# Late mixing weights in pieces of four degrees, and the linear weights moved to the head of SyncE's queue

## What is computed

```python
def _L0_conv_ref(x, w1r, w1i, w2r, w2i):          # w*: (32 in, 32 out, 32 degrees, 32 orders)
    w1 = jax.lax.complex(w1r, w1i)
    x_ft = _sht(x)                                # Fourier over longitude, Legendre over latitude
    top = jnp.einsum('bixy,ioxy->boxy', x_ft[:, :, :M1, :M2], w1)
    bot = jnp.einsum('bixy,ioxy->boxy', x_ft[:, :, -M1:, :M2], w2)
    ...
    return _isht(out_ft)

x = x + _L0_conv_ref(_ln_c(x), w1r, w1i, w2r, w2i)
x = x + _L0_ffn_ref(_ln_t(x))                     # an opcode layer
x = x + _L1_conv_ref(_ln_c(x), lin_w, lin_b, bn_g, bn_b, bn_m, bn_v)   # spiking attention
x = x + _L1_ffn_ref(_ln_t(x), Wg, bg, W1, b1, W2, b2)                  # eight experts, two a token
```

## Time and profile before

| | |
|---|---|
| median of 3 runs | 1313.02 us (1310.09 to 1319.51) |
| the profiled execution | 1314.89 us, of which the span is 1313.1 us |
| TensorE matmul busy | 993.3 us (76%) |
| VectorE busy | 859.5 us (65%) |
| ScalarE busy | 654.5 us (50%) |
| GpSimd busy | 565.4 us (43%) |
| mean granted TensorE clock | 0.849 |

### The profile page before, as it was taken

One profiled execution on the slowest core, in us unless ns is written; L12 is line 12 of the kernel. 1 busy time (PEld: TensorE's weight loads), 2 busy tenths in 40 slices (PEclk: granted clock), 3 DMA queues, 4 the chain that ended last, 5 costly groups with the idle time before them and its releaser, 6 DMA issues. The chain is left out here.

```text
span 1313.1 us, 23822 instructions
## 1 busy us (share of the span) xinstructions
PE 993.3 (76%) x6645; PEld 837.2 (64%) x6646; DVE 859.5 (65%) x2743; ACT 654.5 (50%) x1400; POOL 565.4 (43%) x731
## 2 busy tenths in 40 slices
PE   9948654876666775768676344089999999999997
PEld 7838653654545654656565233078888888888886
DVE  7716533675578898897984753256666676666665
ACT  3428641445859768676855421134444444444443
POOL 3310000110231566656664667535555555555554
PEclk9979876987778878787787555589999999999999
DMA  9996947780011010000000001111111111111110
GB/s 269 221 247 137 255 108 191 191 185 20 20 38 32 20 44 24 26 16 24 19 17 27 22 22 35 34 43 45 43 46 49 40 49 47 45 49 49 46 38 2
DMA packets 103604, 93.12 MB, mean 71 GB/s; under 512 B 7884, under 2 KB 92236, under 8 KB 102761
## 3 DMA queue, kind: packets, MB, share of 16 engines
q1 hardware_dynamic: 74905, 62.02, 19.6%
q0 software_dynamic: 9088, 17.33, 4.0%
q10 hardware_dynamic: 19536, 12.85, 3.8%
HBM read 55.61 MB, written 38.39 MB: 72 GB/s over the span
## 5 line engine op out<-in xcount | busy, mean ns | idle before, releaser
L1686 POOL DMA_INDIRECT out_dram<-res,index x156 | 156.0, 1000 | 218.0 <-DVE res L1769 190.0
L1816 ACT ACTIVATE sil<-ps_h 128x512 f32<-128x512 f32 x156 | 93.1, 597 | 255.0 <-PE ps_h L1868 255.0
L1734 DVE TENSOR_TENSOR act_rows<-ps_h,sil 128x512 f32<-128x512 f32 x156 | 107.9, 692 | 132.9 <-ACT sil L1816 132.9
L1887 PE MATMUL ps_y<-r_raw,aT 128*128 x1248 | 164.8, 275 | 0.0
L158 POOL DMA_INDIRECT slots<-x_sb,r_pos x128 | 130.9, 1023 | 54.2 <-issue 33.2
L1887 PEld LDWEIGHTS ps_y<-r_raw,aT 128*128 128x128 f32 x1248 | 151.6, 192 | 0.1
L1866 PE MATMUL ps_h<-wp,uTh 128*128 x312 | 137.6, 441 | 1.6 <-DVE uTl L1728 1.6
L1867 PE MATMUL ps_h<-wp,uTh 128*128 x312 | 124.7, 400 | 0.0
L1868 PE MATMUL ps_h<-wp,uTl 128*128 x312 | 123.1, 395 | 0.0
L1057 PE MATMUL ps_q<-wqkv,zT 128*128 128x256 f32 x256 | 114.2, 538 | 0.0
L1169 POOL TENSOR_TENSOR x_sb<-x_sb,sy 128x256 f32<-128x256 f32 x64 | 43.8, 684 | 138.0 <-ACT sy L1305 137.8
(11 more groups left out here) (242 smaller groups left out, 2465.4 us busy)
## 6 DMA issues: line engine op xcount, KB each, us to landing
slots<-zero SPq DMA_DIRECT2D x4, 2652.0 KB, 23.2
pay<-slots SPq DMA_DIRECT2D x39, 272.0 KB, 2.8
wc<-in_L_conv_w1r SPq DMA_DIRECT2D x4, 1024.0 KB, 15.1
wc<-in_L_conv_w1i SPq DMA_DIRECT2D x4, 1024.0 KB, 20.3
wc<-in_L_conv_w2r SPq DMA_DIRECT2D x4, 1024.0 KB, 21.7
wc<-in_L_conv_w2i SPq DMA_DIRECT2D x4, 1024.0 KB, 22.3
coefc<-coefficients ACTq DMA_DIRECT2D x16, 256.0 KB, 6.6
mixed<-mo ACTq DMA_DIRECT2D x16, 256.0 KB, 7.1
```

The source lines that it names most:

```text
L1686: nc.gpsimd.indirect_dma_start(out_rows, bass.IndirectOffsetOnAxis(at, 0), res[:, m % RES, :], None, bounds_check=TOKENS - 1, oob_is_err=F ...
L1734: nc.vector.tensor_tensor(act_rows[:, k], ps_h[:, k, :, DFF:], sil[:, k], ALU.mult).then_inc(s_act, 1)
L1816: nc.scalar.activation(sil[:, k], ps_h[:, k, :, 0:DFF], ACT.Silu).then_inc(s_sil, 1)
L1887: ins = nc.tensor.matmul(dst, aT[:, k, (2 * e + h) * P:(2 * e + h + 1) * P], raw[:, 4 + h, col], start=(h == 0), stop=(h == 1))
```

## The change

Chunks 2 and 3 are no longer loaded in 8 degrees each, but as four loads of 4 degrees each, one for each of the steps 4 to 7. The load for step n goes into the half slot that step n-4 has used, and is issued once step n-4 is mixed. Each is four DMAs of 512 KB; the runs in DRAM are 512 B. Each step has a semaphore of its own. The first two chunks are loaded as before. The load of `lw` moves from ScalarE's program to the head of SyncE's in the synthesis block.

```diff
+        s_wq = [sem(f"mix_weights_late_{k}") for k in range(WS * LW // LQ)]
+        w_late = [w.rearrange("i o (k l) m -> k i o (l m)", l=LQ) for w in spectral_w]
...
+        def load_late(eng, n):
+            k = n % (WS * LW // LQ)
+            at = n * LQ % LW
+            for g in range(4):
+                eng.dma_start(wc[32 * g:32 * g + 32, k * LQ // LW, :, at:at + LQ, :].rearrange("i o l m -> i o (l m)"), w_late[g][n])\
+                    .then_inc(s_wq[k], 16)
...
-                    for c in range(WS, L2 // LW):
-                        sp.wait_ge(s_mm, (c - WS + 1) * (LW // LQ))
-                        load_w(sp, c)
+                    for n in range(WS * LW // LQ, NCH):
+                        sp.wait_ge(s_mm, n - WS * LW // LQ + 1)
+                        load_late(sp, n)
...
-                        c = n * LQ // LW
-                        pe.wait_ge(s_w[c % WS], c // WS * 64 + 64)
+                        if n < WS * LW // LQ:
+                            pe.wait_ge(s_w[n * LQ // LW], 64)
+                        else:
+                            pe.wait_ge(s_wq[n - WS * LW // LQ], 64)
...
             @block.sync
             def _(sp):
+                sp.dma_start(lw[:, :, :], t["L1_conv_lin_w"].rearrange("i d c -> d i c")).then_inc(s_load, 16)
                 sp.dma_start(psyn[:, :, :], ...)
...
             @block.scalar
             def _(act):
-                act.dma_start(lw[:, :, :], t["L1_conv_lin_w"].rearrange("i d c -> d i c")).then_inc(s_load, 16)
```

## The result

The changed kernel takes 1299.45 us (median of 7 runs, 1295.97 to 1304.97), the kernel before, run beside it, 1316.12 (7 runs, 1310.09 to 1319.51): ratio 0.9883, 95% interval [0.9852, 0.9914]. Run again on another chip, the same pair gave 0.9933 [0.9908, 0.9959]. For that repeat I had expected 0.988, mixing of 81 us and 10.3 us for the last step; it gave 78.7 and 9.0. The medians differ by 16.7 us in the first pair and by 8.2 in the second; the profiled executions (span 1313.1 before, 1300.8 after) differ by 12.3.

What follows compares the result with a forecast made beforehand. The late weight stream was taken to bound the mixing block, and waits headed by `lw` the synthesis block. Gains of 6.5 us in mixing and 5.7 in synthesis, 12.2 together, took 1313.02 to 1300.8 us, range 1294 to 1309.

Steps and rivals of the forecast that it cites:

- Earlier start: Mixing block, late weight stream: bytes run from 111.0, 7.6 us earlier, as the first late load follows step 0.
- Rate: Late weight stream in 512 B runs: 165 GB/s taken, 150 to 177 allowed, against 192 for 1 KB runs.
- the rival in which the rate hardly falls: Late weight stream: 177 GB/s or more; time 1294.4 at 192 GB/s, 1295.8 at 177; chance 27%.
- What it shares with: Late weight stream: five coefficient loads fall into it and cost 10.5 us; ScalarE's stores cost nothing.
- Landing: Mixing block: the last late load lands at 172.3 us, 1 us later than before.
- One step behind it: Mixing block, after the last load: one step instead of two, 9.3 us after an idle, ending at 181.6.
- ScalarE's loop as the next bound: Mixing block, if weights are early: ScalarE's loop ends it at 175.2 at the earliest, gain at most 12.9 us.
- Waits of VectorE and ScalarE for their own DMAs: Mixing block: new meetings with a full queue cost nothing; without cover, 1 to 3 us once.
- Linear weights: Synthesis block: `lw` first on SyncE, 2 to 4 us in flight; line 664 starts at 211.0 to 211.4, 5.7 us gained.
- The chances: Whole kernel, against a bound of about 1%, 13.1 us: faster 0.42, same 0.54, slower 0.04.

Runs made afterwards that it cites:

- old triggers: Changed kernel, but pieces for steps 4 and 5 issued once step 1 is mixed, 6 and 7 once step 3 is; ratio 0.9913 to the kernel before.
- two kernels with weights in time: Changed kernel with step 4's weights in their own place, loaded at block start (0.9884 to before); changed kernel with late DMAs to all 128 partitions (0.9881).
- GpSimd's queue: Changed kernel, but GpSimd issues two of each late piece's four DMAs, to the other partition half or the same; ratios to before 0.9909 and 0.992.
- the later fifth piece: Changed kernel plus a place for step 4's weights, loaded once the first two steps' coefficients landed, steps 5 to 7 one step earlier; ratio to before 0.991.
- the runs of 1 KB: Changed kernel with the weights' place in four pieces, each 512 KB DMA taking 16 output channels of 8 degrees; ratio to before 0.9865.
- late weights only: Kernel before with the late weights in pieces of four degrees, `lw` left on ScalarE's queue; ratio to before 0.9942.
- linear weights only: Kernel before with `lw` moved to the head of SyncE's queue, late weights in 1 MB DMAs as before; ratio to before 0.9953.

## Why the prediction was right, step by step

The forecast was 1300.8 in 1294 to 1309 and the measured 1299.45 lies in it; for the gain foreseen, 12.2 us, the medians show 16.7 in the first measurement and 8.2 in the second, the profiled pair 12.3. The mechanism was right: the last landing and the one step behind it end the mixing, and `gin` instead of `lw` opens the synthesis. That the sum came out so near is in part luck. In the mixing block the start came 0.5 us later than foreseen, the better rate took 3.4 us off, the sharing put 1.6 on and the last step 1.0, and these all but cancel (the block's last matmul ended at 181.38, 181.6 foreseen). The total's 1.4 us lie far inside the 8 us by which unchanged code varies.

- *Earlier start.* Foreseen 8.6 us after step 0's start, measured 9.9 (110.20 - 100.30). TensorE stayed longer at its lower clock in step 0 (granted 0.74 over it, 0.80 before). This is small, but the prediction took step 0 as a warm one plus a fixed rest.
- *Rate.* The mis-sized term: 165 GB/s foreseen, 177 to 185 measured. That is at or over the upper end of 150 to 177, outside of which the prediction called itself wrong, and it is the condition of the rival in which the rate hardly falls. That rival's gain of 17.2 to 18.6 us did not come: its landing at 165.2 to 168.9 was missed because the start came later and the sharing took more, and its warm last step because the clock fell. The fit blamed all of the difference between 1 KB and 8 KB runs on a cost per run, 1.0 ns. From 177 to 185 GB/s for 512 B and 192 for 1 KB, both to 32 partitions, the same working gives 0.2 to 0.5 ns a run (an estimate); what else sets the long runs of `gin` apart, no run here shows. The figure worked out from the Trainium skill's cycles a packet ("DMA: Bandwidth & Descriptors", section "Why small descriptors are slow (HBM only)"), an estimate of 177, was met.
- *What it shares with.* From about 111.5 to 171.06 the stream took 59.5 us; 8.39 MB at 177 are 47.4, so five coefficient loads and the stores took 12.1, where 10.5 stood in the sum. It cancelled part of the better rate.
- *Landing.* 172.3 foreseen, 171.06 measured. A wait of 1.61 us was left before step 6, where the prediction had none before steps 4 to 6.
- *One step behind it.* 9.3 us foreseen, 10.3 and 9.0 in two runs. The mixing gain came out at 6.0 us for 6.5 in the first pair, 8.4 in the second. The prediction credited the early start with paying for the slower rate. The run with old triggers has mixing at the same 81.1 us, since its last step kept the clock, so the early start paid 0 to 3 us there and not the 4.7 that its expectation gave it.
- *ScalarE's loop as the next bound.* 12.9 us at most below 87.1, so 74.2; two kernels with weights in time took 74.8 and 74.9.
- *Waits of VectorE and ScalarE for their own DMAs.* Costed at nothing, and they did not decide here. They did with GpSimd's queue, with the later fifth piece, and with the runs of 1 KB, where the weights were in time and mixing still took 77.4 us.
- *Linear weights.* 5.7 us foreseen, 6.6 in the first pair. `lw` was 3.1 us in flight (2 to 4). `gin`'s first group landed 15.2 us after the opening instead of 16.6; I had expected `lw` ahead of it to push it by 0.5. Before, ScalarE's 524 packets stood between SyncE's large ones in that stretch, but they are not shown to be the cause: with late weights only, where `lw` is still ScalarE's, the group landed 15.6 us after the opening (issued at 189.36, 12.9 us in flight, opened at 186.65), and with linear weights only 15.7. The spread between executions covers the difference.
- *The chances.* Faster by over 1% had 0.42. The first measurement says 1.17%, the second 0.67%: the bound runs through what was measured.

## What to carry to other kernels

Where a stream of loads sets the end of a stage, ask first how much work stands behind the last landing: cutting the last pieces in half brought 6 to 7.6 us in the one run that has it alone, and starting them 7 us earlier 0 to 3, although the cut cost 7% of the rate. Read the granted clock of the last step beside its landing: with a landing 3 us earlier, step 7 ran at the lower level and took 2.9 us longer. A small load that heads a chain of small work goes to the front of the queue, ahead of the megabytes that are needed later: `lw` took 3.1 us there and 18.6 beside them. When a stream is made faster, look at what it shares the DMA engines with: VectorE's waits for ScalarE's stores took back part of the gain in three kernels here.

## What had not been expected of the hardware

- A DMA to 32 partitions and one to 128, with the same runs of 512 B from the same places, moved 182 and 288 GB/s.
- Three queues with packets of unlike size moved nearly equal numbers of packets in the same 5 us (251, 269, 272), and so 0.96 MB for the one with packets of 3.8 KB against 0.14 MB each for the two with packets of 512 B.
- After a wait of 3.00 us TensorE kept its full clock and after one of 2.19 us, in the same execution, it was granted the lower level when work resumed.
- The part of the program that no kernel here changes took 1075.6 to 1083.7 us in fourteen executions, so a stage's own marks, which repeat to about 2.5 us in the mixing block, tell what the totals of this kernel don't.
